# A two-layer graph transformer on one core: two normed buffers, and the split of a step's normed blocks at the step's end

## The reference

```python
# layer 0
nx = ln(x, ln1_g, ln1_b);  q, k, v = nx @ wq + bq, nx @ wk + bk, nx @ wv + bv      # 8 heads of 32
scores = q @ k.T / sqrt(32) + where(adj > 0, 0.1 * adj * adj, -inf)
x1 = x + (softmax(scores) @ v) @ wo + bo
x2 = x1 + gelu(ln(x1, ln2_g, ln2_b) @ w1 + b1) @ w2 + b2                            # 1024 hidden
# layer 1
q, k, v = x2 @ Wq + bq, x2 @ Wk + bk, x2 @ Wv + bv
y = softmax(where(adj == 0, -inf, q @ k.T / sqrt(32))) @ v @ Wo + bo + x2
out = ln(y) * gamma + beta
```

## Time and profile before

| | us |
|---|---|
| median of 3 runs (lowest to highest) | 2387.24 (2386.19 to 2387.51) |
| the profiled execution, device time | 2387.25 |
| its span, first to last instruction | 2384.8 |
| PE busy | 2208.7 |
| DVE busy | 1960.2 |
| ACT busy | 1700.4 |
| POOL busy | 1095.8 |

### The profile page before, as it was taken

The page is one execution under the profiler, slowest core; times in us unless marked ns, Lnnn a source line. Parts: engine busy times, 40 slices in busy tenths (PEclk is TensorE's granted clock), DMA queues, the critical chain, the costliest instruction groups (busy, mean ns, idle before and its releaser), DMA issues.

```text
span 2384.8 us, 62848 instructions
## 1 busy us (share of the span) xinstructions
PE 2208.7 (93%) x22336; PEld 1924.1 (81%) x22336; DVE 1960.2 (82%) x8492; ACT 1700.4 (71%) x5646; POOL 1095.8 (46%) x1159
## 2 busy tenths in 40 slices
PE   4699999999999999999999999999999999999986
PEld 4588888888888888888888888888888888888875
DVE  4588888888888888888888888888888888888775
ACT  2477777777777777777777777777777777777773
POOL 0234544554444455444454454554454455444444
PEclk8799999999999999999999999999999999999988
DMA  3011111111101111101111101111101111110010
GB/s 113 18 33 46 32 33 35 46 42 43 39 28 32 46 46 40 45 22 34 44 46 39 46 24 41 35 46 39 46 31 34 35 46 40 45 38 29 24 33 25
DMA packets 98930, 92.77 MB, mean 39 GB/s; under 512 B 8640, under 2 KB 94272, under 8 KB 98624
## 3 DMA queue, kind: packets, MB, share of 16 engines
q1 hardware_dynamic: 98624, 88.77, 12.1%
HBM read 55.20 MB, written 16.78 MB: 30 GB/s over the span
## 4 chain that ended last, share of the span: by engine, by line
PE 69%; DVE 18%; ACT 8%; issue 4%; POOL 0%; POOLq 0%; DVEq 0%; ACTq 0%
PE p_bank L1007 53%; PE p_heads L1106 7%; DVE normed L793 5%; ACT scores L573 5%; PE p_heads L1092 4%; DVE x_two L686 3%; PE p_bank L1126 3%; DVE scores L773 2%; DVE stats_C L672 1%; PE p_bank L1025 1%; DVE probs_t L834 1%; DVE res_c L851 1%; ACT normed L584 1%; ACT queries_a L587 1%; ACT probs_t L603 1%
## 5 line engine op out<-in xcount | busy, mean ns | idle before, releaser
L523 POOL TENSOR_TENSOR scores<-scores,inverse 128x512 f32<-128x512 f32 x512 | 537.8, 1055 | 715.7 <-DVE inverse L783 715.7
L573 ACT ACTIVATE scores<-scores,negmax 128x128 f32<-128x128 f32 x2048 | 794.9, 393 | 62.6 <-DVE negmax L773 62.2
L573 ACT ACTIVATION_READ_ACCUMULATOR scores<-scores,negmax 128x1 f32 x2048 | 393.1, 192 | 0.0
L1007 PE MATMUL p_bank<-normed,w_up 128*128 128x512 f32 x1536 | 370.1, 397 | 21.7 <-DVE normed L793 21.7
L1007 PE MATMUL p_bank<-w_down,hidden 128*128 128x256 f32 x3072 | 381.4, 284 | 0.0
L1007 PEld LDWEIGHTS p_bank<-w_down,hidden 128*128 128x128 f32 x3072 | 374.2, 190 | 8.6 <-issue 6.0
L1007 PEld LDWEIGHTS p_bank<-normed,w_up 128*128 128x128 f32 x1536 | 285.5, 189 | 89.0 <-issue 29.5
L1106 PE MATMUL p_heads<-ident,scores 128*128 128x128 f32 x2048 | 313.1, 277 | 17.9 <-DVE negmax L773 17.5
L834 DVE COPY probs_t<-p_heads 128x512 f32<-128x512 f32 x256 | 176.0, 687 | 134.1 <-PE p_heads L1106 134.0
L594 ACT ACTIVATE p_bank<-p_bank,ready_cols 128x512 f32<-128x512 f32 x256 | 169.5, 662 | 154.1 <-PE p_bank L1007 148.9
L1106 PEld LDWEIGHTS p_heads<-ident,scores 128*128 128x128 f32 x2048 | 245.0, 142 | 42.0 <-DVE negmax L773 20.3
(11 more groups left out here) (113 smaller groups left out, 3820.2 us busy)
## 6 DMA issues: line engine op xcount, KB each, us to landing
x_in<-in_x SPq DMA_DIRECT2D x32, 512.0 KB, 3.8
res_a<-in_x SPq DMA_DIRECT2D x32, 512.0 KB, 4.0
res_c<-x_two SPq DMA_DIRECT2D x32, 512.0 KB, 3.3
out<-res_c SPq DMA_DIRECT2D x128, 128.0 KB, 1.7
adj_a<-in_adj SPq DMA_DIRECT2D x32, 256.0 KB, 3.7
adj_c<-in_adj SPq DMA_DIRECT2D x32, 256.0 KB, 2.8
res_c<-in_L_gnn_w SPq DMA_DIRECT2D x1, 512.0 KB, 6.1
values_c<-in_L_gnn_w SPq DMA_DIRECT2D x1, 512.0 KB, 7.0
```

The lines of the kernel that those rows point to most:

```text
L523: nc.gpsimd.tensor_tensor(rows_c, rows_c, inverse[:, k % 2, heads].unsqueeze(2).broadcast_to([P, HC, P]), ALU.mult).then_inc(probs_made, 1)
L573: last = nc.scalar.activation(scores[:, k % 2, h], scores[:, k % 2, h], ACT.Exp, scale=-1.0, bias=negmax[:, k % 2, h:h + 1], accum_out=tot ...
L1007: last = nc.tensor.matmul(dst, stationary(i), moving(j), start=(n == 0), stop=(n == total_n - 1))
```

## The change

The change has five parts.

1. There are two `normed` buffers, used in turn. XT of M moves from the head of step 3 into step 2, XT of C from the head of step 5 to the end of step 4, and XT of the next group's A (called N) from the head of step 0 to step 7 of the pass before. The new list `ahead` holds them: behind both halves of T and behind W on PE, behind the step's exponentials on ACT, behind the residual on DVE, and ahead of the step's `fill`.
2. K, Q and UP wait for each chunk's split just ahead of the products that read it.
3. Mean, variance and root of the M stage are made block by block, as for C; blocks 0 and 1 are normalised in step 0, block 2 in step 1, block 3 in step 2.
4. The DMA `res_c<-x_two` and its semaphore go. POOL reads `x_two` itself as it adds the bias row, at the head of step 0 and no more in step 1.
5. The number of a PSUM bank follows the new order.

```diff
-        self.late, waiting = {}, []
+        self.late, waiting = {}, [-3] if pending else []
...
-        self.first = {0: [("XT", "A")] * a, 3: [("XT", "M")] * m, 5: [("XT", "C")] * m}
+        self.first = {0: [("XT", "A")]} if before is None else {}
+        self.ahead = {2: [("XT", "M")] * m, 4: [("XT", "C")] * m, 7: [("XT", "N")] * (a and following)}
...
+    def normed_room(self, what):
+
+        return (self.it + (what in "MN")) % 2
...
-                if s.m:
-                    if s.c:
-
-                        sp.wait_ge(stored, (t.group_c + 1) * GB * 16)
-                    if not (s.a and s.c):
-                        sp.wait_ge(*drained_use(t, ("DOWN", 1)))
-                    sp.dma_start(res_c[:, :, :], x_two[:, :, :]).then_inc(res_c_loaded, 16)
...
                     if op == "W":
                         _, stage, b = t.unit(r)
-                        if stage == "A" and b == GB - 1:
-                            make_rstd("M", 0, GB, t.group(r) * 3 + 3)
-                        if stage == "C":
-                            make_rstd("C", b, b + 1, (t.group(r) * GB + b) * 3 + 3)
+                        make_rstd("M" if stage == "A" else "C", b, b + 1, (t.group(r) * GB + b) * 3 + 3)
...
-                x = res_c if stage == "C" else res_a
+                x, src = (res_c, x_two) if stage == "C" else (res_a, res_a)
...
+                    if k == 0 and s.c:
+
+                        wait(pool, stored, t.group_c * GB * 16)
+                        bank, number = t.bank(("DOWN", 1), earlier=True)
+                        add_bias("C", drained[bank], number)
...
-                if stage == "C":
-                    layer_norm_steps("C", x, b, b + 1, (group * GB + b) * 3, True)
-                else:
-                    last = nc.vector.bn_stats(stats["M"][:, b, :], x[:, b, :])
-                    if b == GB - 1:
-                        last.then_inc(ln_steps["M"], 1)
-                        layer_norm_steps("M", x, 0, GB, group * 3, False)
+                layer_norm_steps("M" if stage == "A" else "C", x, b, b + 1, (group * GB + b) * 3)
...
-                elif b == GB - 1:
-
-                    wait(dve, res_c_loaded, group * 16)
-                    normalize("M", res_a, x_two, 0, GB, group + 1)
+                else:
+                    for b_ in {1: (0, 1), 2: (2,), 3: (3,)}.get(b, ()):
+                        wait(dve, biased["C"], group * 2 - (b_ < 2))
+                        normalize("M", res_a, x_two, b_, b_ + 1, group * GB + b_ + 1)
...
                     for _, r in only("W", lag):
                         add_residual(t, r)
+                    for op in s.ahead.get(k, []):
+                        evacuate(t, op)
...
+            def split_of(t, what, c):
+
+                earlier = what == "A" and t.s.before is not None
+                bank, number = t.bank(("XT", "N" if earlier else what, c), earlier=earlier)
+                return drained[bank], number
...
                     for _, r in only("T", lag):
                         turn(t, r, 1)
+                    for op in s.ahead.get(k, []):
+                        work(t, op)
                     for op in s.fill.get(k, []):
                         work(t, op)
```

More of the change, by code:

```diff
@@ L118, in __init__ @@
             self.number(self.first.get(k, []) + only("V", lag) + self.early.get(k, [])
-                        + self.mid.get(k, []) + only("W", lag) + self.fill.get(k, []))
+                        + self.mid.get(k, []) + only("W", lag) + self.ahead.get(k, []) + self.fill.get(k, []))
             if k == self.steps[-1]:
@@ L231, in build @@
         half, fence, table_turn = sb("half", [P, GB]), sb("fence", [P, 16]), sb("table_turn", [P, 1])
-        normed = sb("normed", [P, 2, KC, TOK], F32R)
+        normed = [sb(f"normed{i}", [P, 2, KC, TOK], F32R) for i in range(2)]
         queries = {"A": sb("queries_a", [P, 2, KC, TOK], F32R), "C": sb("queries_c", [P, 2, KC, TOK], F32R)}
@@ L583, in evacuate @@
                     if kind == "XT":
[L584 removed]
+                        nc.scalar.activation(normed[t.normed_room(what)][:, HI, use[2], :], src[:, :], ACT.Copy
+                                             ).then_inc(high_made, 1)
                     elif kind in "QK":
@@ L666, in take_wait, with layer_norm_steps @@
                 nc.vector.memset(fence[:, at_col:at_col + 1], 0.0)
-            def layer_norm_steps(n, src, b0, b1, done, measure):
-                if measure:
-                    for b in range(b0, b1):
-                        last = nc.vector.bn_stats(stats[n][:, b, :], src[:, b, :])
-                    last.then_inc(ln_steps[n], 1)
+            def layer_norm_steps(n, src, b0, b1, done):
+                for b in range(b0, b1):
+                    last = nc.vector.bn_stats(stats[n][:, b, :], src[:, b, :])
+                last.then_inc(ln_steps[n], 1)
                 dve.wait_ge(ln_steps[n], done + 1)
@@ L1067, in hidden_split @@
                 return drained[bank], number
-            def wait_split(t, what):
-                for c in range(KC):
-                    bank, number = t.bank(("XT", what, c))
-                    pe.wait_ge(drained[bank], number)
             def make_scores(t, k):
```

47 lines of the change are left out of this document (26 added, 21 removed).

## The result

| | before | after |
|---|---|---|
| median of 4 runs each (lowest to highest), us | 2387.38 (2386.19 to 2387.98) | 2328.40 (2326.18 to 2332.69) |
| the profiled execution, device time, us | 2387.25 | 2329.64 |
| its span, us | 2384.8 | 2327.0 |
| a steady pass, XT of A to XT of the next A, us | 71.00 | 69.50 |

The ratio is 0.9756, with a 95% interval of 0.9739 to 0.9773: faster. The time lies 13.4 us under the 2341.8 us that the forecast's sum gives, and inside both ranges.

The account below looks back on a forecast made before the run. PE was taken as the bound, held up by DVE at a few places. 30 passes give 37.5 us and the ends 8, in all 45.5: span 2339.3, with 2.45 outside it 2341.8; own range 2320 to 2359, 8 in 10 2312 to 2366.

Parts of the forecast that it names:

- The path from masking 5 to XT of M: DVE's maskings, ACT's exponentials, residuals and statistics up to XT of M: 37.22 us before, 35.2 after, XT 2.0 sooner.
- The steps: Masking to masking from 5 to 2, then to the normalisation and XT: 6.11, 6.13, 7.3, 6.3, 6.1, 2.8, 0.45 us.
- From XT of M to UP: PE's stretch behind the path: 3.15 us before, 4.0 to 4.1 with V in it; UP 1.25 sooner.
- The steps on the races: DVE against POOL: first normalisations win at 0.39, step 0's second costs about 1.0; bias row covered by 0.2 us.
- The third rival: Slower: normalisations of steps 0, 1 and 2 all lose to POOL, 0.7 a pass lost, 2400 us; chance 0.08.
- The rule on semaphores: Skill page: a semaphore after each DVE instruction costs nothing extra; by it the sum would be some 18 us lower.
- the added 0.41 a step: Mean and variance by block: A0, A1 and A2 each add 0.41 us to DVE between two maskings.
- XT behind T, ahead of V: On PE, V (1.65 us) behind XT covers the waits of 0.49 ahead of K of A and 0.66 ahead of UP.
- The ends: Second pass and last two passes, with waits of 4.53 ahead of K and 1.88 ahead of UP: 8 us gained, bounds 3 and 11.
- XT of M was said to wait some 0.7: PE's remaining wait ahead of XT of M in a steady pass, 1.10 us before.
- About 2 of the 3.24 us of waiting: PE's waits in a steady pass that stay, in new places: ahead of XT of M, K of C (0.4) and in `turn`.

Follow-up runs that it names:

- Statistics twice: The changed kernel with the statistics of each block of M taken a second time into a spare tile; 2362.52 us, 70.57 a pass.
- means later: The changed kernel with mean and variance moved behind the next step's first maskings, except those of steps 3 and 7; 2298.04 us, 68.50 a pass.
- the last version: The changed kernel with means put later, POOL's bias row in step 7 and step 0's two normalisations ahead of its first inverse; 2275.57 us.
- before + both: The kernel before with only the waits by chunk and POOL adding the bias row from x_two at step 0's head; 2328.56 us, 69.24 a pass.

## Why the prediction was right, and where it was off

**The mechanism was right.** The path from masking 5 to XT of M was forecast at 35.2 us and is 35.02, and the pass at 69.75 and is 69.50. The steps, forecast and measured: 6.11 and 6.11; 6.13 and 6.12; 7.3 and 7.23; 6.3 and 6.22; 6.1 and 6.12; 2.8 and 2.78; 0.45 and 0.44. Statistics twice and means later moved the pass by what the path says, in both directions. From XT of M to UP 4.0 to 4.1 was forecast, and it is 3.83, another 0.2 us a pass. The rows give it: V's products take 1.59 from start to start (2040.53 to 2042.12), and V starts 0.85 behind XT where the scores started 1.02 to 1.09 behind it (1026.52 and the end at 1027.61 in the earlier trace rows), so it is 2.49 + 1.59 less some 0.24. One sum was wrong by itself: 2.0 + 3.15 less 4.0 to 4.1 is 1.05 to 1.15, and the prediction took 1.25 of it. So the terms were 0.35 to 0.45 us a pass too small against the measured 1.50, and the slip of 0.1 went the lucky way.

**The steps on the races were right.** The bias row (2.54) starts behind step 7's root and ends ahead of the first inverse, POOL's timeline of after:

```profile
2023.59 2.54 POOL L500 TENSOR_TENSOR res_c<-x_two,row_bias 128x512 f32<-128x512 f32 x2
2026.60 1.14 POOL L522 TENSOR_TENSOR scores<-scores,inverse 128x512 f32<-128x512 f32 x1 [0.47 <-DVE inverse L787]
```

It ends at 2026.13, and the inverse begins at 2026.34: covered by 0.2, as forecast. The pair of normalisations then took 1.45, which is 0.39 for the first, ahead of `make_probs`, and about 1.06 for the second if the first took what a single one takes; the single ones took 0.39. The third rival, slower, asked for three collisions; there is one in a pass (a normalisation of C in step 6 takes 0.65 for 0.39, but it does so in both kernels).

The Trainium skill, SBUF — State Buffer, section SBUF: two separate sides, says that the two engines share a pair of ports as a lock that the first takes for its whole instruction; for VectorE it limits that to some kinds of instruction. The trace agrees in every order that the runs made: 0.73 for a pair with POOL idle, 1.45 for a pair that meets one instruction of POOL, and 2.09 for a pair that meets two.

**The rule on semaphores.** From the statistics to the mean it is 0.47 in after too (2016.13 to 2016.60), with 0.35 where nothing is waited for (before a masking or a split), and the added 0.41 a step was measured as 0.40 (5.72 to 6.12). The Trainium skill, VectorE: DVE Perf Modes, section The DRAIN you can't avoid, found that it cost nothing extra behind each of eight copies; here the difference is 0.12. What follows without a wait is another instruction, one that doesn't read the statistics, so no run here has the same pair with and without the wait.

**XT behind T, ahead of V: right in the numbers, wrong in what it credited.** The prediction said that V gives K of A and UP cover, and the waits did go (0.49 and 0.66 to none). The experiments show that the cover is worth nothing: V between XT and UP costs on the path what it hides. What removed the waits of K of A and UP by themselves was the wait by chunks, which the prediction credited only at K of C. With the bias row's move it is the whole gain of the steady passes, 1.76, and gives 2328.56 us.

**The terms that were mis-sized.** The ends: 8 us were forecast with bounds 3 and 11, and 57.8 us of span less 30 passes at 1.50 leave 12.8, outside the bounds. The second pass shows most of it, PE's timeline of after against the earlier trace rows:

```profile
92.50 2.92 PE L1014 MATMUL p_bank<-normed,w_k 128*128 128x512 f32 x12
...
101.72 11.24 PE L1014 MATMUL p_bank<-normed,w_up 128*128 128x512 f32 x48
```

The same UP before, and three windows of before with the granted clock (the column behind POOL):

```profile
109.37 12.98 PE L1007 MATMUL p_bank<-normed,w_up 128*128 128x512 f32 x48 [1.88 <-DVE normed L793]
...
96.00:98.00 2.00, 1.41 (x3) 1.16 (x4) 0.44 (x1) 0.00 (x0) 1.92 (x2) 0.62 0.05 14
98.00:100.00 2.00, 2.00 (x6) 1.61 (x5) 0.00 (x0) 0.48 (x1) 0.00 (x0) 0.52 0.95 314
...
110.00:112.00 2.00, 2.00 (x7) 1.58 (x6) 0.00 (x0) 0.35 (x1) 0.00 (x0) 0.54 0.00 0
```

K doesn't wait (4.53 before), and its 12 products take 2.92, where they took 4.53 behind that wait, at a granted clock of 0.62 and then 0.52. UP stands at 101.72, against 109.37, 7.65 us sooner, and its 48 products take 11.24 where they took 12.98 behind the wait of 1.88, at a clock of 0.54. The prediction counted the two waits and not the 1.61 and 1.74 us of half clock behind them, together 3.35 us, where its 8 were 4.8 short. By the first DOWN of this pass the gain is 9.40; the other 3.4 lie in the rest of the pass and in the last two, and aren't split further. XT of M was said to wait some 0.7, and waits 0.25: the rest of that waiting falls sooner, in the 0.29 of step 1's scores and in the unmarked gaps. About 2 of the 3.24 us of waiting were to stay, and 1.74 stay (3.24 less 1.50): 0.94 marked and some 0.8 in the gaps. That is read, not tested.

**What it didn't foresee.** The wait of step 1's scores for `probs_t`, 0.29 in most passes. The two normalisations of step 0 stand ahead of the copy of the turned probabilities, so that one starts at 2027.81, 1.47 behind the inverse. I had looked at the 1.06 us that DVE idles ahead of this copy and asked whether the pair fits; I hadn't asked who waits for the copy. In after it costs little: from masking 0 to 1 it is 6.22, where 5.71 and the 0.41 would be 6.12, and with the pair moved ahead of the inverse in the last version 0.10 went from the same place (5.81 to 5.71). It shows more in the versions with means later, as waits of 0.63 and 0.92.

What stays open: what makes the clock fall in 24 passes of 29 behind one and the same wait; which wait of PE gave which part of the 0.49 on the path; and whether means put later would give as much with one buffer.

## What to carry to other kernels

Follow the loop between the engines, from one first masking to the next, to the instruction at its end, and compare sums of that path and of what lies behind it; the list of waits alone names places, not prices. A change of several parts is worth trying part by part even when its sum comes out as forecast: here two small parts gave all of what the steady passes won, and the largest, a second buffer with moved transposes, gave nothing there and some 6 us at the start. Equal times don't mean equal causes: compare the steady pass and the ends apart. When a removed wait has a stretch at the lower clock behind it, count that stretch too. When an instruction moves into idle time ahead of another one, ask who waits for that other one.

## What the runs showed of the hardware that I had not expected

- The granted clock of TensorE fell to 0.50 behind an idle time of 1.92 us in 24 passes of a kernel, and stayed at 1.00 behind the same idle time in 5 others; each fall cost 1.6 us. The idle time of 1.10 us in the same place of before was followed by no fall, in passes of 71.00 throughout. A wait can thus cost more than its own length: with the fall, a pass that was 0.73 us shorter than before (70.27) became 0.86 longer (71.86).
- The start of the second pass shows falls behind other idle times. Before, the clock fell to 0.52 behind an idle time of 4.53 us and, once back at 1.00, to 0.54 behind one of 1.88; the stretches behind them took 1.61 and 1.74 us more than in after. In "before + both" the idle time ahead of the same UP is 1.28 us, the clock stays at 1.00 (107 to 111 us), and the 48 products take 11.24:

```profile
107.46 11.24 PE L1002 MATMUL p_bank<-normed,w_up 128*128 128x512 f32 x48 [1.28 <-DVE normed L788]
```
